# A graph network kernel: block numbers read into registers for four turns at once

## What is computed

```python
# L0, twice: attention over hyperedges
a   = leaky_relu(xt[row] @ att[:H] + et[col] @ att[H:])
alpha = softmax of a over the edges of one col
eout = segment_sum((Binv[col] * stoich * alpha)[:, None] * xt[row], col)
nout = segment_sum((Dinv[row] * stoich * alpha)[:, None] * eout[col], row)
# L1: messages by a two-layer perceptron of x[row], x[col], summed at col
# L2: gated messages with a layernorm, summed at edge_dst
# L3: graph attention with 4 heads, once along and once against the edges
e   = leaky_relu(e_src[src] + e_dst[dst]); att = softmax of e over the edges of one dst
out = segment_sum(h[src] * att, dst)
```

## Time and profile before

| | us |
|---|---|
| median of 3 runs | 15397.82 |
| lowest, highest | 15387.91, 15453.75 |
| span of the profiled execution, first to last instruction | 11824.4 |
| POOL busy | 7882.7 |
| DVE busy | 8065.6 |
| PE busy | 8621.2 |

### The profile page before, as it was taken

One profiled execution on the slowest core, in us unless ns is written; L12 is line 12 of the kernel. 1 busy time (PEld: TensorE's weight loads), 2 busy tenths in 40 slices (PEclk: granted clock), 3 DMA queues, 4 the chain that ended last, 5 costly groups with the idle time before them and its releaser, 6 DMA issues. The chain is left out here.

```text
span 11824.4 us, 190141 instructions
## 1 busy us (share of the span) xinstructions
PE 8621.2 (73%) x50733; PEld 7028.2 (59%) x50733; DVE 8065.6 (68%) x30113; ACT 5189.3 (44%) x14989; POOL 7882.7 (67%) x7789
## 2 busy tenths in 40 slices
PE   7886777788885878656654555688886777767776
PEld 5676767766765777644443555567775454535554
DVE  7665888755556777655554222488887788878888
ACT  3454444433333444322222111266665466646665
POOL 2333777677775777677775777377885677747775
PEclk7766777655556666666656666799998566666666
DMA  1111222255552222377773444255553444434443
GB/s 16 7 19 36 54 54 54 53 126 127 130 129 67 54 54 54 90 198 202 202 191 91 131 130 132 88 155 158 158 157 115 127 134 134 134 108 134 134 134 114
DMA packets 679361, 1297.58 MB, mean 110 GB/s; under 512 B 192850, under 2 KB 335664, under 8 KB 677808
## 3 DMA queue, kind: packets, MB, share of 16 engines
q0 software_dynamic: 282368, 575.57, 22.3%
q1 hardware_dynamic: 355584, 615.03, 16.4%
q10 hardware_dynamic: 40368, 94.82, 2.1%
HBM read 1050.01 MB, written 234.74 MB: 109 GB/s over the span
## 5 line engine op out<-in xcount | busy, mean ns | idle before, releaser
L609 POOL DMA_INDIRECT WK<-tab,IDX x4640 | 4604.1, 992 | 1698.3 <-issue 1390.1
L1429 POOL DMA_INDIRECT B<-tab,IDX x1856 | 1774.8, 956 | 839.2 <-issue 504.5
L921 PE MATMUL PS<-WK 128*128 128x129 f32 x5568 | 1152.4, 371 | 717.9 <-ACT WK L1158 484.2
L921 PEld LDWEIGHTS PS<-WK 128*128 128x128 f32 x5568 | 988.3, 266 | 831.0 <-ACT WK L1158 535.7
L1448 DVE TENSOR_REDUCE WK<-PS 128x4 f32<-128x1024 f32 x928 | 1131.4, 1220 | 189.2 <-PE PS L1574 186.7
L1559 ACT ACTIVATE B<-B 128x33 f32<-128x33 f32 x5568 | 1211.2, 308 | 7.8
L840 ACT ACTIVATE WK<-WK 128x128 f32<-128x128 f32 x1856 | 592.7, 390 | 1236.4 <-DMA WK<-tab,IDX 1223.9
L609 POOL DMA_INDIRECT H<-tab,IDX x928 | 898.7, 968 | 348.2 <-issue 267.5
L1607 PEld LDWEIGHTS PS<-B,H 128*128 128x128 f32 x3712 | 816.2, 328 | 281.6 <-issue 275.7
L1607 PE MATMUL PS<-B,H 128*128 128x132 f32 x3712 | 875.5, 428 | 86.1 <-DVE ACC L1461 86.0
L1574 PE MATMUL PS<-B 27*128 27x512 bf16 x1856 | 725.7, 503 | 131.2 <-DVE WK L1448 126.2
(11 more groups left out here) (425 smaller groups left out, 20098.8 us busy)
## 6 DMA issues: line engine op xcount, KB each, us to landing
H<-onehots SPq DMA_DIRECT2D x232, 768.0 KB
B<-onehots SPq DMA_DIRECT2D x232, 384.0 KB
onehots<-B ACTq DMA_DIRECT2D x232, 384.0 KB
WK<-onehots SPq DMA_DIRECT2D x232, 384.0 KB
WK<-tab,IDX POOLq DMA_INDIRECT x4640
onehots<-WK SPq DMA_DIRECT2D x232, 256.0 KB
WK<-onehots SPq DMA_DIRECT2D x232, 256.0 KB
onehots<-B SPq DMA_DIRECT2D x232, 128.0 KB
```

The lines of the kernel that those rows point to most:

```text
L609: po.indirect_dma_start(out=G[:, g % n, k, :], out_offset=None, in_=table, in_offset=bass.IndirectOffsetOnAxis(ap=IDX[:, idx, t:t + 1], ax ...
L921: mm = pe.matmul(AG(r, k // 2), OH[:, r, k, :], R[:, r % 2, k, 0:129], start=k % 2 == 0, stop=k % 2 == 1)
L1429: po.indirect_dma_start(out=eG[:, g % 4, k, :], out_offset=None, in_=tab[TW3], in_offset=bass.IndirectOffsetOnAxis(ap=IDX[:, o, t:t + 1], ...
```

## The change

`blocks` loads the numbers of four turns (AHEAD = 4) at once, in the first of these turns, and hands out the part of the turn that asks. The registers are kept by engine and lane. As `a_ve` reads numbers for two different turns in one round of its body, `vm` gets a lane of its own. A load brings 8 numbers into registers, 16 in e; 232 and 116 are multiples of four, so all loads are whole. All waits and all other instructions stay in their order.

```diff
+AHEAD = 4
...
-        def blocks(eng, o, g, n=2):
-
-            _, v = nc.values_load_multi_w_load_instructions(
-                BLK[0:1, o, bass.ds(g * n, n)], engines=[eng.engine], min_val=0, max_val=NB - 1,
-                skip_runtime_bounds_check_because="node numbers are below 6250, so blocks are below 49")
-            return v
+        held = {}
+
+        def blocks(eng, o, g, n=2, lane=0):
+
+            first = g - g % AHEAD
+            if g == first:
+                _, held[eng.engine, lane] = nc.values_load_multi_w_load_instructions(
+                    BLK[0:1, o, first * n:min((first + AHEAD) * n, NT // 2)], engines=[eng.engine], min_val=0, max_val=NB - 1,
+                    skip_runtime_bounds_check_because="node numbers are below 6250, so blocks are below 49")
+            return held[eng.engine, lane][(g - first) * n:(g - first + 1) * n]
...
-                    vm = blocks(ve, 0, gm)
+                    vm = blocks(ve, 0, gm, lane=1)
```

## The result

| | before | changed |
|---|---|---|
| median, us | 15420.14 (4 runs) | 15023.94 (4 runs) |
| lowest, highest | 15387.91, 15453.75 | 15019.07, 15059.62 |
| span of the profiled execution | 11824.4 | 15017.3 |

The ratio is 0.9743, with a 95% interval of 0.9719 to 0.9767. The kernel got faster, by 396 us. The forecast was 15410, the range 15310 to 15505.

What follows compares the result with a forecast made beforehand. POOL's gathers and issue gaps were taken to bound the kernel, with waits for ACT in e. Stage ends -9, longer loads +1 and phase in a +22 made +14 us on 15397.8: 15412, given as 15410, range 15310 to 15505.

Steps and rivals of the forecast that it cites:

- The 3573 us: Difference between the profiled span, 11824.4 us, and the timed median, 15397.82; taken as outside the trace and fixed.
- POOL's floor: Four gathers of 0.951 us with 0.305 us gaps take at least 5.02 us a turn, 1165 us per a stage.
- What the change takes away: Three of four loads go; 355 us of VectorE stalls, covered by POOL except at stage ends: -9 us.
- Rival 1: VectorE bounds stages a and d, its stalls are real time and 355 us come out: 15043; chance 0.06.
- d: Stage d, 1359.00 us, set by POOL: gathers with gaps 1181 us, plus 116 insertions of L1215; VectorE's load uncovered before L908.
- Longer loads: Eight values take 0.53 us and sixteen 0.92, nearly all covered, with e the tight case: +1 us.
- Rival 4: A load costs 0.267 us a value, leaving 195 us uncovered in e: 15590; chance 0.06.
- Phase: Earlier VectorE work falls differently against POOL's gathers and lengthens them: +11 us in each a stage, +22 us.
- The tests that I had named: Wrong if a stages fall under 1165 us, e grows beyond 1214 by over 15, or d changes by over 20.
- The two tests on e and d: Wrong if e grows beyond 1214 us by more than 15, or d changes by more than 20 us.
- The counts of loads: After the change, 522 loads on VectorE and 290 on TensorE.

Runs made afterwards that it cites:

- x2: Kernel before with only VectorE reading four turns at once, TensorE loading every turn: ratio 1.0004 against before at 11807.33 us.
- x4: Changed kernel with eight turns read at once on both engines: ratio 1.0006 against before at 11807.33 us.
- w1: Four turns at once in the a stages alone, with an unread write of zeros in place of each load: ratio 1.0024 against before at 11810.61 us.
- w3: Four turns at once in a alone, only for the accumulation's numbers (w2: only the maximum's, 1.0017): ratio 1.0025 against before at 11810.61 us.
- y2: Changed kernel with four turns at once everywhere but in the a stages: 15191.98 us, ratio 1.0018 against before.
- x1: The kernel before, unchanged, profiled again beside its own timed runs: ratio 0.9996 against before at 11807.33 us.
- x3: Kernel before with only TensorE reading four turns at once, VectorE loading every turn: ratio 0.9997 against before at 11807.33 us.
- z3: Kernel before with six more semaphore increments a turn on TensorE in b, waited for by nobody: 15417.38 us, ratio 0.9999.
- x6: Kernel before, meant to issue each load twice; the second loads are absent from the trace, so it is before once more: ratio 0.9993.
- y4: Kernel before with each group of four TensorE transposes in b made three times over: 15282.40 us, ratio 1.0085.
- y3: Kernel before with one load instruction for each number, 7424 loads in place of 3248: 15127.81 us, ratio 0.9984.
- x5: The changed kernel, unchanged, run again beside the kernel before: 14919.52 us, ratio 0.9851.
- x7: Kernel before with gathers of 32 rows in place of 128, except the first of each ring: 11482.45 us.

## Why the prediction was wrong

- **The 3573 us.** This is the step that failed. I had a span of 11824 us beside a median of 15398, called the difference "outside what the trace shows" and took it as fixed. Nothing of that size lies outside a span: in every run whose span is on record the time is the span and some 2 us. The two numbers were of different executions, and in the profiled one POOL sets the pace in a, which it doesn't in the timed ones. The Trainium skill had a hint of the size: "Runtime: NRT & Kernel Launch", section "The ~15µs preamble/postamble breakdown", gives about 6 us by which a profile's total exceeds the time reported. Here the time reported exceeds the span, by some 2 us; the sign differs, and both are microseconds and not milliseconds. A gap of 3573 us should have been read as "this profile is not of the runs that I predict".
- **POOL's floor.** Right at the short level, and wrong where the timed runs were. At the short level POOL's 0.305 us stand before every gather of a, whatever VectorE does (x2, x4, w1 to w3), and the kernels with fewer loads differ from before by -0.03 to +0.25%. At the long level the a stages are 1494 to 1756 us, 6.4 to 7.6 us a turn against POOL's own 5.0 to 5.2, and POOL waits for DVE.
- **What the change takes away.** The stalls were counted rightly for the short level (0.51 us at L741, rows 6) and dismissed by the floor. Rival 1, "the stalls are real time", was given 0.06 and 15043; the result is 15024. It was right in size, and partly by luck: its 355 us are three quarters of the stalls in a, b, f, c and d, of which a has 325 x 3/4 = 243. The runs show 263 to 343 us out of a and nothing out of b, f, c, d and e together (y2). Of the 396 us of the first measurement no trace of before in the same group tells the stages. Rival 1's stated condition, "executions in which POOL's gap or gathers are shorter", is not what happened either. POOL's work is as long as ever, and it is TensorE's increments that come late, in about every second turn of a, and make the mean turn longer than POOL's floor.
- **d.** I had the load uncovered in d (rows 8). DVE's fastest turns in d do get shorter (fifth percentile of the distances between L908's starts 5.80 us in x1, 5.28 in x2), but the stage doesn't move at either level: 1360 us and 1357 (x2) at the short level, 1795 and 1796 at the long. The prediction's account of its length doesn't add up either: 1181 us and 116 times 1.874 are 1398, 39 more than 1359. The rows fit without the "some 0.2" and with the measured gaps: 899 of gathers, 269 of gaps, 189 of L1215 and 3.
- **Longer loads.** Eight values 0.60 us and sixteen 1.10, against my 0.53 and 0.92. From four values on it is 0.063 us a value over 0.09: 0.34, 0.60, 1.10, 2.11 for 4, 8, 16 and 32. Rival 4's 0.267 a value is gone. The Trainium skill's page "Runtime: NRT & Kernel Launch", section "Instruction fetch mechanics", gives its 200 ns a register for TENSOR_LOAD, which the page describes as loading registers from HBM; the numbers here lie in SBUF, and the traces don't show that rate for them. The term was +1 us; x2's e stages came out 1 to 3 us longer than before's. At 32 values the cover of 0.91 us in e is passed and each e stage loses 13 us.
- **Phase.** The term was +22 us for a. At the short level the a stages took +28 and +4 with four turns at once on DVE (x2), +18 to +23 and +1 to +8 in w1 to w3: the right term, the mean length of a gather, and about the right sum, on one stage rather than both. I had left b and f out; their mean gather fell, by 23 and 16 us over the stage, and so x2 as a whole stands at +4 us. Which operation of VectorE makes the gathers longer no run here varied. The changed kernel itself, with gathers of 128 rows, was never run at the short level; that it would come out within 0.5% of before there rests on its two halves (x2, x3) and on eight turns at once (x4).
- **The tests that I had named.** "Wrong, if the a stages fall under 1165 us" could not catch this: at the long level they are far above that with the change (1570 and 1582 us) and without it (1756 and 1737 in z3, at a like time of before). The two tests on e and d did fire, e at 1737 us and d at 1892 in the changed kernel's profile, but by the level and not by the change. A test on a stage's length needed a trace of before from the same group. The counts of loads were right.

## What stays open

What makes the long level. The traces show where it sits: increments of TensorE that come late, by some 5 us in every second turn of a. From the records of semaphore changes I worked out the delay between the end of a PE instruction that raises a semaphore and the change itself: 0.01 us at the median in every stage at the short level, and over 1 us for half of them or more in a, b, f and c at the long, and for a quarter to under a half in d and e. The latest come 6 us late in a (95th percentile) and 10 to 13 in c and e. VectorE's median stays at 0.01. (At the long level some of the records are missing, so these shares are rough.) The same chip number gave 15173 us in the fourth group and 11811 in the sixth, so it isn't bound to a chip by number. The granted clock doesn't explain it: in the second a it is 0.64 at both levels (x6, rows 2), and the stage takes 1698 and 1191 us. In the first a it is 0.65 against 0.71, in d 0.89 against 0.99. Open too is why d keeps its length when DVE's stall in it goes, and whether other work in place of the loads would bring a's time back.

One suspicion I can't test: recording. The short level's traces hold 201000 records of semaphore changes and the long level's 75000 to 77000, and of DMA landings 164000 and some 48000, for the same program. In the sort, where such changes are few, both hold some 5790 and the sort takes equally long. And there TensorE's increments are on time at the long level too, in the same execution: 208 of them at 0.014 us at the median, none over 0.02 (x6). So they come late only where records are missing. In b there are 30047 at the short level, and 7600 to 8900 at the long whatever the kernel is, 5 to 5.5 a microsecond. The Trainium skill's page "NOTIFIC — the notification-queue block", section "7.1 Overflow: three behaviours, one of which stalls the engine", says that a record queue that is full drops records or, in another mode, stalls the engine that makes them. By the second, the long level would be a price of recording. The traces show both at once, records missing and increments late, so they agree with neither mode alone. That z3, with more increments, was no slower speaks against the number of these records as the cause, and in y4, with more instructions of TensorE, the pauses were no more either (115 against 138), though b got longer. No run here settles it.

## What to carry to other kernels

Before a profile is read, its span has to be set against the timed runs. Here the two agree within 2 us when they are of the same execution; a difference of 3573 us meant that the profile showed another regime, and that its bound need not be theirs; the forecast should then carry both, each with its chance. A stall behind a covering engine is surely worth nothing only while that engine sets the pace: here fewer loads in a gained nothing where POOL set the pace (w1 to w3 took 23 to 28 us longer), and four turns at once gained 263 to 341 us where it didn't. But another engine can stand behind the first, as d shows, so the worth has to be measured stage by stage. Two turns at once, four values a load in a, took nearly all that there was to gain, and a load of 32 values in e went with 13 us lost in each e stage.

## What the runs showed of the hardware

- A register load by its number of values on DVE, medians: 1: 0.306 (y3), 2: 0.530, 4: 0.34, 8: 0.60, 16: 1.10, 32: 2.11 us (x4). Two neighbouring values cost more than four; PE's are the same within 0.03. In b at the long level DVE's take longer, 0.81 us for two values (x6) and 0.87 for eight (x5), and PE's don't; why, no run shows.
- A gather of 32 rows takes 0.867 us of POOL where one of 128 takes 0.951 (c in x7 and in rows 3), so nearly all of it is per gather and not per row.
- The same program at 11.8 and at 15.1 to 15.4 ms, with the same busy time of DVE and POOL within some 2%, and with increments of TensorE that come some 5 us after the matmuls' recorded ends in a and up to 13 us in e.
